# Expert stage of an audio tower: row and quarter tiles of the array for the first two products, batch norm scale folded into the weights, second relu and router weight in one VectorE operation

## The reference

```
w = softmax(mean_over_batch(x) @ Wr + br)            # (token, expert), 8 experts
h = relu(bn1(einsum('bfd,edh->bfeh', x, W1) + b1))   # 64 -> 64, each expert
h = relu(bn2(einsum('bfeh,ehk->bfek', h, W2) + b2))
y = einsum('bfeh,ehd->bfed', h, Wo) + bo
out = residual + einsum('bfed,fe->bfd', y, w)
bn(h) = g * (h - m) * rsqrt(v + 0.001) + b           # per expert and column
```

## Time and profile before

| | us |
|---|---|
| median of 3 runs | 931.92 |
| lowest and highest | 927.72, 933.09 |
| span of the profiled execution | 929.8 |
| mean granted clock of TensorE | 0.958 of 2.4 GHz |

### The profile page before, as it was taken

How to read it: one execution, slowest core, us unless ns; L and a number is a source line. 1 busy time by engine, 2 the same in 40 slices (tenths; PEclk the granted TensorE clock), 3 DMA queues, 4 the chain that set the end, 5 groups by cost and what they waited for, 6 DMA issues and landing times.

```text
span 929.8 us, 9248 instructions
## 1 busy us (share of the span) xinstructions
PE 838.5 (90%) x2430; PEld 364.7 (39%) x2430; DVE 599.8 (65%) x1001; ACT 662.3 (71%) x988; POOL 281.9 (30%) x200
## 2 busy tenths in 40 slices
PE   9898798898798898898998978867999999999997
PEld 5334344344344444433443534423333333333332
DVE  4669679779779778878978947735433333333333
ACT  4876795896887787797697677761566666666664
POOL 7005414606606606506516416612100010000000
PEclk7999998999999999998998999897999999999999
DMA  1000000000000000000000000000000000000001
GB/s 38 1 2 0 1 2 0 1 2 1 1 1 0 0 1 0 0 1 0 0 0 0 0 1 0 1 0 2 12 11 23 11 11 11 22 12 11 11 12 34
DMA packets 11548, 5.56 MB, mean 6 GB/s; under 512 B 2909, under 2 KB 11397, under 8 KB 11525
## 3 DMA queue, kind: packets, MB, share of 16 engines
q1 hardware_dynamic: 10517, 4.66, 1.7%
q0 software_dynamic: 704, 0.55, 0.2%
q10 hardware_dynamic: 304, 0.07, 0.0%
HBM read 1.09 MB, written 4.19 MB: 6 GB/s over the span
## 4 chain that ended last, share of the span: by engine, by line
PE 51%; DVE 22%; ACT 16%; issue 9%; POOL 1%; DVEq 0%; ACTq 0%; POOLq 0%
PE TB L980 11%; PE TB L987 11%; PE TB L734 9%; PE QB L997 6%; DVE Z L1064 5%; DVE M L1136 3%; PE TB L725 2%; DVE NC_ L1153 2%; PE QB L821 2%; DVE K_NN L1194 2%; DVE LF_UT L1130 2%; ACT U L474 2%; DVE AT L1080 2%; ACT UF L482 2%; ACT L562 1%
## 5 line engine op out<-in xcount | busy, mean ns | idle before, releaser
L734 PE MATMUL TB<-U,w2T 128*128 128x512 f32 x448 | 220.7, 636 | 28.2 <-ACT U L474 28.1
L1329 DVE TENSOR_TENSOR Z<-Z,AT 128x512 f32<-128x512 f32 x118 | 82.6, 701 | 173.2 <-ACT Z L695 173.2
L474 ACT ACTIVATE U<-Z 128x512 f32<-128x512 f32 x192 | 114.0, 628 | 78.0 <-DVE Z L1064 77.6
L689 ACT ACTIVATE A<-TB,bn_t,bn_s 128x512 f32<-128x512 f32 x114 | 88.6, 777 | 99.9 <-PE TB L980 95.4
L1064 DVE TENSOR_TENSOR Z<-TB,A 128x512 f32<-128x512 f32 x224 | 142.3, 682 | 12.8 <-PE TB L734 12.5
L734 PEld LDWEIGHTS TB<-U,w2T 128*128 128x128 f32 x448 | 86.6, 202 | 148.4 <-issue 86.3
L980 PE MATMUL TB<-XN,fw 128*128 (+1 forms) x228 | 112.1, 614 | 0.6 <-DVE LF_UT L1319 0.6
L987 PE MATMUL TB<-A,fw 128*128 128x512 f32 x228 | 107.1, 592 | 0.0
L376 POOL TENSOR_TENSOR KZ<-K_NN,side 128x1024 f32<-128x1024 f32 x16 | 33.5, 2117 | 235.1 <-DVE K_NN L1119 235.1
L442 POOL TENSOR_TENSOR SQ<-HH,LF_UT 128x512 f32<-128x512 f32 x16 | 21.9, 1372 | 246.6 <-DVE XC_IS L1336 234.0
L695 ACT ACTIVATE Z<-TB,bn_t,bn_s 128x512 f32<-128x512 f32 x114 | 88.6, 777 | 10.9 <-PE TB L987 1.8
(11 more groups left out here) (208 smaller groups left out, 1310.0 us busy)
## 6 DMA issues: line engine op xcount, KB each, us to landing
result<-V SPq DMA_DIRECT2D x32, 128.0 KB, 1.8
X<-in_x SPq DMA_DIRECT2D x8, 32.0 KB
fw<-in_ffn_W POOLq DMA_DIRECT2D x2, 128.0 KB, 2.9
fw<-in_ffn_W POOLq DMA_DIRECT2D x2, 64.0 KB, 2.6
fwo<-in_ffn_Wo POOLq DMA_DIRECT2D x2, 64.0 KB, 2.3
wproj<-in_attn_Wg SPq DMA_DIRECT2D x6, 16.0 KB
SQL<-in_tok_b SPq DMA_DIRECT2D x4, 0.5 KB
wac<-in_tok_W SPq DMA_DIRECT2D x2, 1.0 KB
```

What stands on the lines that cost most here:

```text
L474: nc.scalar.activation(U3[:, 2 * j:2 * j + 2, 1:UW], Z3[:, 2 * j:2 * j + 2, :], ACT.Relu)\
L689: nc.scalar.activation(H1[t % 2][:, k, :], TB[k][:, :], ACT.Relu, bias=bn_t[:, 0, t % EP:t % EP + 1], scale=bn_s[:, 0, t % EP:t % EP + 1]) ...
L734: pe.matmul(TB[j][:, :], w2T[:, :], U3[:, 2 * j:2 * j + 2, 0:T], start=True, stop=True)\
L1329: nc.vector.tensor_tensor(v, v, WM[:, t % EP, :].unsqueeze(1).to_broadcast([P, 2, T]), ALU.mult)\
```

## The change

- First products: the weights of a pair lie on both halves of the partitions (fw1 loses one dimension), and for each k a product of 64 rows and 128 columns reads only the partitions of sequence k. Two row tiles write two banks.
- Second products: four products of 64 x 64 in place of two of 128 x 128; expert e of sequence k goes to `half[e ^ k]` of bank k. For k = 1 the two experts lie swapped, and so do their third weights (fwo_sw), router weights (WM[1]) and shifts (t2_pos, t2_neg). The second products alternate between the bank pairs TB[2:4] and QB[2:4]; QB[0] takes all third products and QB[1] all transpositions.
- The scale g * rsqrt(v + eps) is folded into the columns of fw1 and fw2 between turns 1 and 2: SP loads v and g broadcast to all partitions, ScalarE takes the logarithm and exponential, VectorE multiplies.
- In the loop ScalarE has only the first relu (a bias, no scale). VectorE computes max(x, -shift) * w from PSUM in one operation; what is missing, shift * w, goes through Wo once for all as a part of BOW (fwo_t, four more products). For the pieces run ahead ScalarE adds the shift and applies the relu, and VectorE takes the shift off and multiplies.
- The router weights leave PSUM in one copy of four banks, and two more copies on half the partitions make WM[1].
- The loops over groups of the expert stage are written out on PE, DVE, ACT and POOL.

```diff
-        fw1 = sb("fw1", [P, 2, EP, P])
+        fw1 = sb("fw1", [P, EP, P])
...
+        fwo_sw = sb("fwo_sw", [P, EP, D])
+        fwo_t = sb("fwo_t", [P, EP, P])
...
+        t2_pos = sb("t2_pos", [P, 2, EP])
+        t2_neg = sb("t2_neg", [P, 2, EP])
...
+            for dst, vs in ((v_rows, (v1, v2)), (g_rows, (g1, g2))):
+                for i, v in enumerate(vs):
+                    sp.dma_start(dst[:, 512 * i:512 * i + 512],
+                                 v.rearrange("(a e) h -> a (e h)", a=1).to_broadcast([P, E * D]))\
+                        .then_inc(rows_loaded, 16)
...
-            nc.gpsimd.memset(fw1[:, :, :, :], 0.0).then_inc(w_cleared, 1)
...
+                pool.dma_start(fwo_sw[half[1 - h], :, :], wov[h]).then_inc(ffn_loaded, 16)
...
+            act.wait_ge(rows_loaded, 64)
+            nc.scalar.activation(v_rows, v_rows, ACT.Ln, bias=BN_EPS).then_inc(rows_ln, 1)
+            act.wait_ge(rows_ln, 1)
+            nc.scalar.activation(v_rows, v_rows, ACT.Exp, scale=-0.5).then_inc(rows_rs, 1)
...
+            act.wait_ge(b["w_out"], 1)
+            nc.scalar.activation(WM[1][half[0], :, :], WM[0][half[1], :, :], ACT.Identity).then_inc(b["ws_out"], 1)
+
+            for t in range(N_AHEAD, 2 * EP * G):
+                i = t - N_AHEAD
                 for k in range(2):
...
+                    act.wait_ge(b["l1_mm"], 2 * i + k + 1)
+                    nc.scalar.activation(H1[t % 2][:, k, :], TB[k][:, :], ACT.Relu,
+                                         bias=bn_t[:, 0, t % EP:t % EP + 1]).then_inc(b["h1"], 1)
...
+            def experts_in(t, banks, done):
+                for k in range(2):
+                    c = HC * (t // EP)
+                    pe.matmul(banks[k][:, :], fw1[half[k], t % EP, :], XN2[half[k], c:c + HC], start=True, stop=True)\
+                        .then_inc(done, 1)
+
+            def experts_mid(t, banks, done):
+                for k in range(2):
+                    for e in range(2):
+                        mm = pe.matmul(banks[k][half[e ^ k], :], fw2[half[e], t % EP, D * e:D * e + D],
+                                       H1[t % 2][half[e], k, :], start=True, stop=True)
+                    mm.then_inc(done, 1)
+
             def ahead_step(i, done=0):
...
+                if i < N_AHEAD:
+                    after(pe, ahead["h1"], 2 * (done + i))
+                    experts_in(i, TB[0:2], ahead["l1_mm"])
+                if i > 0:
+                    j = i - 1
+                    pe.wait_ge(ahead["h1"], 2 * (done + j) + 2)
+                    after(pe, ahead["h2"], 2 * (done + j))
+                    experts_mid(j, TB[2:4], ahead["l2_mm"])
...
+            def bias_out():
+                pe.wait_ge(b["wt_out"], 1)
+                pe.wait_ge(folded, 3)
+                pe.matmul(QB[3][:, 0:T], bo_w[:, :], wt, start=True, stop=False)
+                for p in range(EP):
+                    mm = pe.matmul(QB[3][:, 0:T], fwo_t[:, p, :], WM[0][:, p, :], start=False, stop=(p == EP - 1))
+                mm.then_inc(b["bo_mm"], 1)
+
+            def l1(t):
+                i = t - N_AHEAD
+                after(pe, b["h1"], 2 * i)
+                experts_in(t, TB[0:2], b["l1_mm"])
+
+            def l2(t):
+                i = t - N_AHEAD
+                pe.wait_ge(b["h1"], 2 * i + 2)
+                pe.wait_ge(b["hw"], 2 * t - 2)
+                experts_mid(t, (TB[2:4], QB[2:4])[t % 2], b["l2_mm"])
+
+            def l3(t):
+                F, p = t // EP, t % EP
+                if p == 0:
+                    after(pe, b["res"], F)
+                pe.wait_ge(b["hw"], 2 * t + 2)
...
-                    mm = pe.matmul(QB[f][half[k], :], fwo[:, p, :], src[:, k, :],
+                    mm = pe.matmul(QB[0][half[k], :], (fwo, fwo_sw)[k][:, p, :], src[:, k, :],
                                    start=(p == 0), stop=(p == EP - 1))
...
+            N_T = 2 * EP * G
+            l1(N_AHEAD)
+            bias_out()
+            for t in range(N_AHEAD - 1):
+                l3(t)
+            turn_out(0)
+            for t in range(N_AHEAD + 1, N_T + 2):
+                if t < N_T:
+                    l1(t)
+                if t - 1 < N_T:
+                    l2(t - 1)
+                l3(t - 2)
+                if t % EP == 3:
+                    turn_out((t - 2) // EP - 1)
+            turn_out(2 * G - 1)
...
+            for e in range(2):
+                for k in range(2):
+                    nc.vector.tensor_copy(t2_pos[half[e ^ k], k, :], bn_t[half[e], 1, :]).then_inc(t2_ready, 1)
+            dve.wait_ge(t2_ready, 4)
+            nc.vector.tensor_scalar(t2_neg[:, :, :], t2_pos[:, :, :], -1.0, None, ALU.mult).then_inc(t2_ready, 1)
             dve.wait_ge(ffn_loaded, 16 * N_FFN)
+            dve.wait_ge(rows_rs, 1)
+            nc.vector.tensor_tensor(v_rows, v_rows, g_rows, ALU.mult).then_inc(rows_out, 1)
+            dve.wait_ge(rows_out, 1)
+            for i, w in enumerate((fw1, fw2)):
+                w = w[:, :, :].rearrange("q p c -> q (p c)")
+                nc.vector.tensor_tensor(w, w, v_rows[:, 512 * i:512 * i + 512], ALU.mult).then_inc(folded, 1)
+            for p in range(EP):
+                mm = nc.vector.tensor_scalar(fwo_t[:, p, :].rearrange("q (t d) -> q t d", t=2),
+                                             fwo[:, p, :].unsqueeze(1).to_broadcast([P, 2, D]),
+                                             bn_t[:, 1, p:p + 1], None, ALU.mult)
+            mm.then_inc(folded, 1)
...
+            nc.vector.tensor_copy(WM[1][half[1], :, :], WM[0][half[0], :, :]).then_inc(b["ws_out"], 1)
+            dve.wait_ge(b["ws_out"], 2)
+
+            def weigh(t):
+                if t >= N_AHEAD:
+                    bank, v, op = (TB[2:4], QB[2:4])[t % 2], H2[t % 2], ALU.max
+                else:
+                    bank, v, op = None, H2_AHEAD[t], ALU.add
                 for k in range(2):
...
+                    nc.vector.scalar_tensor_tensor(out=rowsof(v[:, k, :]), in0=rowsof(bank[k] if bank else v[:, k, :]),
+                                                   scalar=t2_neg[:, k, t % EP:t % EP + 1],
+                                                   in1=WM[k][:, t % EP, :].unsqueeze(1).to_broadcast([P, 2, T]),
+                                                   op0=op, op1=ALU.mult).then_inc(b["hw"], 1)
...
+            for t in range(2 * EP):
+                weigh(t)
+                if t == 1:
+                    dve.wait_ge(b["bo_mm"], 1)
+                    nc.vector.tensor_copy(BOW, QB[3][:, 0:T]).then_inc(b["bo_out"], 1)
+                if t == EP:
+                    finish(0)
+                if t == EP + 2:
+                    token_major(0)
+            for t in range(2 * EP, 2 * EP * G):
+                weigh(t)
+                if t % EP == 0:
+                    finish(t // EP - 1)
+                if t % EP == 2:
+                    token_major(t // EP - 1)
+            finish(2 * G - 1)
+            token_major(2 * G - 1)
```

More of the change, by code:

```diff
@@ L353, in _ @@
             for h in range(2):
[L354 removed]
+                pool.dma_start(fw1[half[h], :, :].rearrange("d p (e h) -> d (p e) h", e=2),
                                W1.rearrange("e d h -> d e h")).then_inc(ffn_loaded, 16)
@@ L438, in _ @@
             pool.wait_ge(b["bo_out"], 1)
-            def residual(g):
-                for f in range(2):
-                    after(pool, b["res"], 2 * g - 1 + f)
-                    nc.gpsimd.tensor_tensor(rowsof(R1[f]), rowsof(hh(g, f)),
-                                            BOW.unsqueeze(1).to_broadcast([P, 2, T]), ALU.add).then_inc(b["res_a"], 1)
-            residual(0)
-            with pool.Fori(1, G) as g:
-                residual(g)
+            for F in range(2 * G):
+                after(pool, b["res"], F - 1)
+                nc.gpsimd.tensor_tensor(rowsof(R1[F % 2]), rowsof(HH[:, HC * F:HC * F + HC]),
+                                        BOW.unsqueeze(1).to_broadcast([P, 2, T]), ALU.add).then_inc(b["res_a"], 1)
         @block.scalar
@@ L492, in ahead_step @@
                         nc.scalar.activation(H1[i % 2][:, k, :], TB[k][:, :], ACT.Relu,
-                                             bias=bn_t[:, 0, i % EP:i % EP + 1],
-                                             scale=bn_s[:, 0, i % EP:i % EP + 1]).then_inc(ahead["h1"], 1)
+                                             bias=bn_t[:, 0, i % EP:i % EP + 1]).then_inc(ahead["h1"], 1)
                 if i > 0:
@@ L499, in ahead_step @@
                         nc.scalar.activation(H2_AHEAD[j][:, k, :], TB[2 + k][:, :], ACT.Relu,
-                                             bias=bn_t[:, 1, j % EP:j % EP + 1],
-                                             scale=bn_s[:, 1, j % EP:j % EP + 1]).then_inc(ahead["h2"], 1)
+                                             bias=t2_pos[:, k, j % EP:j % EP + 1]).then_inc(ahead["h2"], 1)
             def turn(it, mix, att, late, plain=False):
@@ L969, in _ @@
             mm.then_inc(b["wt_mm"], 1)
```

(44 more changed lines are left out.)

126 lines of the change are left out of this document (37 added, 89 removed).

## The result

| | before | after |
|---|---|---|
| median, us | 932.5 (927.72 to 940.28, 4 runs) | 855.67 (855.26 to 864.11, 4 runs) |
| span of the profiled execution | 929.8 | 853.8 (its own time 855.58) |
| mean granted clock | 0.958 | 0.946 |

The ratio is 0.918, 95% interval 0.9125 to 0.9238: 8.2% faster. Of two versions further down one run each (853.22 and 847.92 us) lies over 1.5% above the fastest of the same kernel, in a slower state of the chip, and is left out of their medians.

The account below looks back on a forecast made before the run. TensorE alone was taken to set the expert loop, the main stretch. Terms -86.2 (the loop) + 4.5 (a) - 3.4 (b) + 1.7 (c) - 0.6 (d) = -84.0, from the median 931.92: 848 us, range 832 to 880.

Parts of the forecast that it names:

- the loop: Expert loop, 56 steps: tiled first and second products cut the step from 4.64 to 3.10 us, giving -86.2 us.
- the transposition: In the expert loop, one transposition (L1009) every fourth step adds some 0.48 us.
- (a): Folding between turns 1 and 2: VectorE runs late and delays turn 2's first layer; +4.5 us, 2.3 to 6.5.
- (b): Pieces run ahead in the last turns: five blocks on the chain get shorter; -3.4 us, bounds 0 and -6.
- (c): Start of the experts: router-weight copies, a swapped copy, weighings not shortened, more bias products; +1.7 us, 0 to 4.
- (d): The end: last second products one block shorter, last weighing slightly longer; -0.6 us.
- (e): One memset less and two loads more on GpSimd, four broadcasts of 256 KB on SP: counted at nothing.
- rival 1: Expert loop: row tiles writing the same bank hold each other up, second products take 1.81; 892 us, chance 0.07.
- 2: Expert loop: waiting lets only the middle pair of second products overlap, or none; 940 or some 987 us, chance 0.04.
- 3: Expert loop: row tiles don't overlap, columns do, so no gain there; 936 us, chance 0.04.
- 4: Code without loops: TensorE stops once per transposition, 14 times, +24 us; 872 us, chance 0.03.
- 5: The clock falls to its lower level in the expert loop, a step of 6.2; 1,020 us, chance 0.02.

Follow-up runs that it names:

- Folding on GpSimd: The changed kernel with all VectorE's folding multiplications, those for the bias term too, moved to GpSimd behind its part of turn 2: 852.29 us, ratio 0.9134.
- The experiment with the new order: The changed kernel with first products of steps 8 and 9 and second of step 7 issued between the third products run ahead: 852.05 us, ratio 0.9137.

## Why the prediction was right, and where it was off

**The bound and the loop: right.** TensorE alone set the loop, and it still does; the blocks are 1.06, 1.02 and 1.01 where I put 1.05, 1.04 and 1.01. The step is 3.085, not 3.10. The two experiments with whole blocks show that each tiling is worth 45 to 50 us of the loop, and no other part of the change comes near. Before, both engines waited for TensorE, so the relu and the multiply taken off them bought nothing by themselves, as forecast. That they had to go for the two to keep up is argued and was not run: before, ScalarE had four operations of 0.777 us in a step (L689, L695 on the page), 3.11 together, more than the 3.085 of the step now. TensorE waited for neither in the loop, with 0.66 us between the end of the relus and the next first products (707.28 and 707.94), and not at a step of 2.89 either.

**The loop's missed term: the transposition.** I took it over at 0.48 us. In the kernel before, the whole-array first products followed it in the same shape; now a shape change stands on both sides. 13.03 - 4 x 3.085 = 0.69, +0.2 each, 14 times +2.8: all that the loop fell short but for the step's -0.9 and rounding. The term of the loop's sum that failed is "a transposition adds some 0.48 us", which I did not work out anew. The experiment with whole first products shows it: there the transposition is back at 0.58 with a block of 1.81 behind it in place of 1.91.

**(a) Folding: right in place, under-sized.** The work behind which turn 2 waits is the one named: ScalarE's two operations to 120.43, then VectorE's 1.23, 1.29, 0.87 on the rows. The first layer is 8.56 us behind the relu of HH, 4.66 before: +3.9, near the forecast. Then the first layer of turn 2 took 3.78 us in place of 1.99, and in that turn TensorE's records show its lower level for some 13.6 us, before for 6.8. That is the upper bound of the prediction (6.5, "if TensorE loses clock in the pause"), and it came: TensorE had stood still for 3.83 us just before. The table under "Folding on GpSimd" bears this out, as far as one execution of each version can: no wait, no fall at this place; a wait of about 1 us, 3.4 us at the lower level; 3.8 us or more, 6.8. What the shorter stretch saves is not to be seen, though: with VectorE's share moved away the layer came 3.0 us earlier and turn 2 took 3.0 less, and from the layer on both took 2.5 us longer than the kernel before.

**Ahead of turn 2: +1.9, not predicted.** There TensorE's code is the same. It ran longer at its lower level between 45 and 56 us (mean clock 0.53, before 0.84). Two of the experiments have the same relu at 111.23 and 110.98, the changed kernel and the other seven at 115.87 to 116.83, the one before at 114.72. One kernel's code so moves by more than the difference, which I put down to the execution and not to the change.

**(b) Pieces ahead: the size right, by luck in part,** -4.0 against -3.4, or -3.5 within the prediction's borders. It counted five blocks on the chain of the kernel before and overlooked a sixth, L802 at 627.38, at the lower level. And it took the chain to stay: in the changed kernel only two blocks of the ahead work are left on it, both first products, and no second ones (start, length, tile, line, count; first the kernel before, then the changed one):

```profile
627.38 3.33 PE TB L802 x4
...
556.00 1.06 PE TB L772 x4
...
560.91 1.11 PE TB L772 x4
```

So 13.9 us of such blocks became 2.2, and other work on the chain took 8 of the 11.7 us back, at a mean clock of 0.84 (before 0.88) from the relu of HH to the copies of the router weights. How these 8 divide was not tested.

**(c) The start of the experts: mis-sized,** +3.9 (+3.4 within the prediction's borders) against +1.7, within its bounds of 0 to 4. A pair of weighings takes 1.42 us alone and 2.42 beside GpSimd's residual (650.47, with POOL's L439 beside). Before it was 1.28 and 2.35, for two pairs; now GpSimd starts later (650.63, before 642.67), so that three pairs lie beside it. TensorE waited 1.26 for one of them, and at the end its clock was 0.53 (windows), so that the last third products took 1.9 and the transposition 1.06. The experiment with the new order puts a number on it: filling the waits gives 3.55 back, more than the term's excess.

**(d), (e) right.** The end gave 0.9, for 0.6. SP's queue delayed nothing: the first use of X in turn 1 is at 47.58 us, 47.75 before.

**The rivals.** 1 and 2 fell: four quarters, two row tiles in each bank, take 1.02 us; two waves would need 1.81. The rule that stood behind rival 1 (the Trainium skill, "TensorEngine Tiling (Array Packing)", Gotcha 1: PSUM Pressure) doesn't hold in this form for two row tiles that write different partitions of one bank. Whether it holds where both write the same partitions wasn't tried, and the version with quarter tiles for the third products avoids it with two banks. 3 fell: the row tiles overlap, 1.06 for the first block. 4 fell: there is no pause without a releaser in the loop (182.55 busy of 182.55). 5 fell: clock 1.00.

**The size of the miss.** Of 8.0 us between sums, 2.2 are the loop, 2.2 the start, 2.0 folding, 2.5 clock and small change up to turn 8, less 0.9 for (b) and (d). The three terms that came out dearer than forecast all lie where TensorE stands still or changes shape. The forecast stands on the loop; that the rest came out so near is helped by (b), whose chain was not the one forecast.

## What to carry to other kernels

When small products are tiled, count the shape changes of the array and not the instructions: one tile shape for all blocks of a loop was worth another 0.5 us of a 3.085 us step, and cutting products finer to reach it cost nothing that shows. What stood between the steps took part of it back: four steps with a transposition fell by 1.41 us, 0.35 a step. Work done once on an engine that the next stage waits for costs its length (3.9 us of start here) and can cost more behind it (2.5 us here, at a lower clock); put it on an engine that is idle there, and fill the waits of a start-up with products of later steps. And when a bound engine is made faster, work out anew what stands between its blocks (here a transposition), since it keeps none of its old neighbours.

## What the runs showed of the hardware

- Beside column tiles, row and quarter tiles also run at once in float32. Behind a block of four products of 64 x 64 on 512 columns the next starts after 0.86 us, as long as two passes on the whole array at 0.43 (four take 1.72). Two row tiles of 64 x 128 take 1.06 between blocks of other shapes, two whole-array products there 1.91.
- A change of the tile shape costs about 0.15 to 0.2 us: three in a step 0.50 (3.085 - 2.58), two 0.31 (2.885 - 2.58), none 0. In the kernel before two cost 0.33 (1.82 + 1.81 + 1.00 less 4.30, ten passes of 0.43). The Trainium skill, "TensorEngine Tiling (Array Packing)", Key Properties, says that a change of mode drains the engine; the traces agree in that every change costs time, and give it this price.
- Two row tiles write different partitions of one bank at the same time without a wait: four quarters in two banks take 1.02 us in either order of issue, between blocks of other shapes.
- A stretch of identical code for TensorE moves by up to 5.8 us between executions with its granted clock (the relu of HH at 110.98 and 116.83). In the profiled execution of the kernel without folding this hid an edit of 2.8 us, which only the rows at the place showed.
- VectorE is slower beside GpSimd: a pair of its operations on two inputs in SBUF, 128 x 512 each, took 2.42 us and 1.42 alone.
